# Gate weights carried with the slot rows, and gathers that add into the tokens by DMA, in a graph and mixture-of-experts kernel

## The reference, cut to what matters

```
r      = layernorm(x)
shared = gelu(r @ W1s + b1s) @ W2s + b2s
rw     = softmax(r @ Wr)                        # 8 experts
topw, topi = top_k(rw, 2);  topw /= sum(topw)   # two gate weights per token
routed = sum over the two experts e of topw[e] * (gelu(r @ W1p[e] + b1p[e]) @ W2p[e] + b2p[e])
x      = x + shared + routed
# then: layer norm, two graph attentions of layer 1, last feed-forward stage
```

## Time and profile before

| | |
|---|---|
| median of 3 runs | 1152.54 us (1150.32 to 1153.1) |
| the profiled execution | 1151.04 us |
| its span, first to last instruction | 1149.3 us |
| PE, DVE, ACT, POOL busy | 85%, 66%, 59%, 41% of the span |
| mean granted TensorE clock | 0.948 of full speed |
| POOL's 128 gathers | 1.00 us each on POOL |
| DVE's 71 bias additions | 0.424 us each |

### The profile page before, as it was taken

The page is one execution under the profiler, slowest core; times in us unless marked ns, Lnnn a source line. Parts: engine busy times, 40 slices in busy tenths (PEclk is TensorE's granted clock), DMA queues, the critical chain, the costliest instruction groups (busy, mean ns, idle before and its releaser), DMA issues. The chain is left out here.

```text
span 1149.3 us, 25194 instructions
## 1 busy us (share of the span) xinstructions
PE 982.7 (85%) x7932; PEld 817.2 (71%) x7980; DVE 758.6 (66%) x2314; ACT 678.8 (59%) x1670; POOL 476.0 (41%) x474
## 2 busy tenths in 40 slices
PE   1788888888899999999999925888898998559998
PEld 1577777777677799999999913565665665349997
DVE  4689999987551144455455422687887886559998
ACT  5455656654333446666666612786877888457774
POOL 2555555552064564444300056665676632111111
PEclk9889999998899999999999966998999999769999
DMA  7901100001624136766656411110110100001111
GB/s 203 360 2 39 38 37 37 36 30 60 168 71 127 51 109 189 206 197 192 196 173 176 119 46 44 30 33 23 34 32 25 33 10 1 1 0 29 37 37 46
DMA packets 91706, 94.15 MB, mean 82 GB/s; under 512 B 16336, under 2 KB 69712, under 8 KB 90448
## 3 DMA queue, kind: packets, MB, share of 16 engines
q1 hardware_dynamic: 71936, 50.40, 14.0%
q10 hardware_dynamic: 11472, 25.63, 8.0%
q0 software_dynamic: 8192, 16.79, 4.7%
HBM read 52.54 MB, written 33.96 MB: 75 GB/s over the span
## 5 line engine op out<-in xcount | busy, mean ns | idle before, releaser
L1552 POOL DMA_INDIRECT g_y<-slot_rows_out,slots x128 | 128.3, 1002 | 149.3 <-SPq L1981 99.0
L1287 POOL DMA_INDIRECT slot_rows_in<-xn_all,slots x128 | 126.4, 988 | 133.1 <-DMA slot_rows_in<-xn_all,slots 83.9
L1174 ACT ACTIVATE s_hT<-s_hp,expert 128x256 f32<-128x256 f32 x284 | 113.1, 476 | 70.4 <-PE s_hp L1165 61.3
L1187 PE MATMUL s_yp<-w_experts,s_hT 128*128 x1136 | 138.4, 275 | 0.3 <-issue 0.3
L1187 PEld LDWEIGHTS s_yp<-w_experts,s_hT 128*128 128x128 f32 x1136 | 132.9, 192 | 0.7 <-issue 0.6
L1195 DVE TENSOR_TENSOR xnT_all<-s_yp,expert 128x256 f32<-128x256 f32 x71 | 30.1, 424 | 116.2 <-PE s_yp L1187 85.1
L491 DVE SCALAR_TENSOR_TENSOR l_mi<-l_sbc,mT 128x512 bf16<-128x512 f32 x128 | 86.2, 684 | 11.9 <-PE l_sbc L482 9.6
L1163 PE MATMUL s_hp<-e_xh,e_wh 128*128 128x256 f32 x284 | 85.9, 302 | 0.0
L1086 ACT ACTIVATE s_hT<-s_hp,b_shared 128x512 f32<-128x512 f32 x64 | 44.0, 687 | 65.1 <-PE s_hp L1069 54.8
L1165 PE MATMUL s_hp<-e_xh,e_wl 128*128 128x256 f32 x284 | 80.1, 282 | 0.0
L1164 PE MATMUL s_hp<-e_xl,e_wh 128*128 128x256 f32 x284 | 80.1, 282 | 0.0
(11 more groups left out here) (324 smaller groups left out, 2660.2 us busy)
## 6 DMA issues: line engine op xcount, KB each, us to landing
expert<-expert_rows ACTq DMA_DIRECT2D x65, 322.0 KB
slot_rows_in<-zeros SPq DMA_DIRECT2D x9, 1024.0 KB, 12.4
xnT_all<-slot_rows_in SPq DMA_DIRECT2D x71, 128.0 KB
slot_rows_out<-xnT_all SPq DMA_DIRECT2D x71, 128.0 KB
xn_all<-l_xr SPq DMA_DIRECT2D x16, 256.0 KB, 2.3
xnT_all<-l_rT SPq DMA_DIRECT2D x16, 256.0 KB
out_dram<-f_ot SPq DMA_DIRECT2D x16, 256.0 KB, 2.3
w_experts<-in_L_ffn_W2p_dram SPq DMA_DIRECT2D x8, 256.0 KB, 3.8
```

The lines of the kernel that those rows point to most:

```text
L1174: nc.scalar.activation(hT[q % 2][:, c, :], hp[:, c, 0:TILE], ACT.Gelu, bias=wt[q][:, F + c:F + c + 1]).then_inc(s["h_ok"], 1)
L1187: ins = pe.matmul(yp[q % 2][:, h * D:(h + 1) * D], hT[q % 2][:, c, h * P:(h + 1) * P], w2, start=(c == 0 and h == 0), stop=(c == FC - 1), ...
L1287: pool.indirect_dma_start(k.rows_in, bass.IndirectOffsetOnAxis(ap=k.slots[:, c, b:b + 1], axis=0), k.xn[:, b, :], None).then_inc(scattered ...
L1552: pool.indirect_dma_start(y_slot[c][:, b, :], None, k.rows_out, bass.IndirectOffsetOnAxis(ap=k.slots[:, c, b:b + 1], axis=0))\
```

## The change

- **Rows.** A row of `k.xn` and of `slot_rows_in` grows from 128 to 132 elements (`ROW`), 528 bytes. Elements 128 to 130 of a token's row hold its first expert, the difference of its two gate weights, and the second gate weight. The last is memset to 0 on POOL.
- **Weights.** ACT takes the exponential after its first two groups of the shared expert, and DVE computes the weights there, between the prefix product's input and its result.
- **Expert rows.** The fetched expert row gets one more element, the expert's number.
- **Tile loop.** DVE gets two small instructions for each tile (`dve_weights`), which pick for each slot the first or the second weight, and the bias addition becomes two instructions: add into `e_y_sum`, then multiply by the weight into the tile. `sp_load` waits for `y_ok` of the tile that had the buffer before, instead of its transposes.
- **Graph stage.** The gathers add into `k.x` in the DMA. The order is all four first rows of a group, then all four second rows, still with two in flight. `dve_n_combine` and the two row buffers go, and `dve_n_stats` waits for the gathers.

```diff
+ROW = D + 4
-            sp.dma_start(k.xn[:, bass.ds(g * GB, GB), :], xr[:]).then_inc(s["xr_kept"], 16)
+            sp.dma_start(k.xn[:, bass.ds(g * GB, GB), 0:D], xr[:]).then_inc(s["xr_kept"], 16)
-    k.zero_dmas = 9
+    k.zero_dmas = -(-72 * 2 * ROW // 2048)
-FETCHED = F + FC + D
+FETCHED = F + FC + D + 1
...
-            wait(sp, s["tp_ps"], t - U + 1)
+            wait(sp, s["y_ok"], t - U + 1)
...
+        def dve_weights(dve, i, q):
+            t = i * U + q
+            wait(dve, x_in[q], i * 16 + 16)
+            wait(dve, w_in[q], i * 16 + 16)
+            wait(dve, s["y_ok"], t)
+            dve.scalar_tensor_tensor(of_first[:], xt[q][:, :, D], wt[q][:, FETCHED - 1:FETCHED], xt[q][:, :, D + 1],
+                                     ALU.is_equal, ALU.mult).then_inc(s["weigh"], 1)
+            wait(dve, s["weigh"], 2 * t + 1)
+            dve.tensor_tensor(w_slot[:], of_first[:], xt[q][:, :, D + 2], ALU.add).then_inc(s["weigh"], 1)
+
         def dve_bias(dve, i, q):
             t = i * U + q
             wait(dve, s["y_ps"], t + 1)
+            dve.tensor_tensor(y_sum[:], yp[q % 2][:, 0:H * D].rearrange("p (h d) -> p h d", h=H),
+                              wt[q][:, F + FC:F + FC + D].unsqueeze(1).to_broadcast([P, H, D]), ALU.add)\
+                .then_inc(s["y_sum"], 1)
             wait(dve, out[q], i * 16)
-            dve.tensor_tensor(yt[q], yp[q % 2][:, 0:H * D].rearrange("p (h d) -> p h d", h=H),
-                              wt[q][:, F + FC:FETCHED].unsqueeze(1).to_broadcast([P, H, D]), ALU.add)\
+            wait(dve, s["weigh"], 2 * t + 2)
+            wait(dve, s["y_sum"], t + 1)
+            dve.tensor_tensor(yt[q], y_sum[:], w_slot[:].unsqueeze(2).to_broadcast([P, H, D]), ALU.mult)\
                 .then_inc(s["y_ok"], 1)
...
+            dve_weights(dve, i, q)
             dve_bias(dve, i, q)
...
+                pool.memset(k.xn[:, :, D + 3:ROW], 0.0)
...
+                act.wait_ge(s["lead"], 1)
+                nc.scalar.activation(lead[:], lead[:], ACT.Exp).then_inc(s["lead_exp"], 1)
...
+                dve.tensor_copy(k.xn[:, :, D], which[:, 0])
+                dve.wait_ge(s["lead_exp"], 1)
+                fold(dve.tensor_scalar(share[:], lead[:], 1.0, None, ALU.add))
+                fold(dve.reciprocal(share[:], share[:]))
+                fold(dve.tensor_tensor(k.xn[:, :, D + 2], lead[:], share[:], ALU.mult))
+                dve.tensor_tensor(k.xn[:, :, D + 1], share[:], k.xn[:, :, D + 2], ALU.subtract)
...
+                dve.tensor_copy(k.b_experts[:, :, FC + D], em8[:])
...
-        y_slot = [sb(f"y{c}", [P, BATCHES, D]) for c in range(TOPK)]
...
-                pool.indirect_dma_start(y_slot[c][:, b, :], None, k.rows_out,
-                                        bass.IndirectOffsetOnAxis(ap=k.slots[:, c, b:b + 1], axis=0))\
-                    .then_inc(gathered[g % 2][c], 16)
+                pool.indirect_dma_start(k.x[:, b, :], None, k.rows_out,
+                                        bass.IndirectOffsetOnAxis(ap=k.slots[:, c, b:b + 1], axis=0),
+                                        compute_op=ALU.add).then_inc(gathered[g % 2][lane], 16)
...
-            if on["n"]:
-                dve_n_combine(dve, g + 4, half + 2, p, 0)
             if on["b"]:
                 dve_b_rden(dve, g + 2)
-            if on["n"]:
-                dve_n_combine(dve, g + 4, half + 2, p, 1)
```

More of the change, by code:

```diff
@@ L814, in _ @@
                 for c in range(k.zero_dmas):
-                    sp.dma_start(rows[:, 2048 * c:2048 * c + 2048], k.zeros[:]).then_inc(k.slots_zeroed, 16)
+                    at = slice(2048 * c, min(2048 * c + 2048, 72 * 2 * ROW))
+                    sp.dma_start(rows[:, at], k.zeros[:, 0:at.stop - at.start]).then_inc(k.slots_zeroed, 16)
                 sp.wait_ge(k.slots_zeroed, 16 * k.zero_dmas)
@@ L917, in add_expert_buffers @@
     k.expert_rows = nc.dram_tensor("expert_rows", [EXPERTS, P, FETCHED], F32, kind="Internal").ap()
-    k.b_experts = buffer(nc, ctx, "b_experts", [P, EXPERTS, 4 + 128])
-    k.expert = [buffer(nc, ctx, f"expert{q}", [P, 512 + 4 + 128]) for q in range(6)]
+    k.b_experts = buffer(nc, ctx, "b_experts", [P, EXPERTS, FETCHED - F])
+    k.expert = [buffer(nc, ctx, f"expert{q}", [P, FETCHED]) for q in range(6)]
     k.expert_in = [ctx.enter_context(nc.semaphore(f"expert_in{q}")) for q in range(6)]
@@ L973, in experts_phase @@
         top = sb("r_top", [P, 2, BATCHES])
+        lead, share = sb("r_lead", [P, BATCHES]), sb("r_share", [P, BATCHES])
         which = sb("r_which", [P, 2, BATCHES])
@@ L1006, in experts_phase @@
         wt, w_in = k.expert, k.expert_in
-        xt = [k.xnT[:, H * q:H * q + H, :] for q in range(U)]
-        yt = [k.xnT[:, H * (U + q):H * (U + q) + H, :] for q in range(U)]
+        slot_rows = k.xnT[:].rearrange("p b t -> p (b t)")
+        XT, YT = H * ROW, H * D
+        xt = [slot_rows[:, q * XT:q * XT + XT].rearrange("p (h d) -> p h d", h=H) for q in range(U)]
+        yt = [slot_rows[:, U * XT + q * YT:U * XT + q * YT + YT].rearrange("p (h d) -> p h d", h=H) for q in range(U)]
+        y_sum, of_first, w_slot = sb("e_y_sum", [P, H, D]), sb("e_of_first", [P, H]), sb("e_w_slot", [P, H])
         xh, xl = [[sb(f"e_x{c}{p}", [P, TILE], F32R) for p in range(2)] for c in "hl"]
@@ L1021, in experts_phase @@
             "sh_ps", "sh_ok", "sy_ps", "sy_read", "fold",
-            "tp_ps", "xh_ok", "xT_ok", "wh_ok", "wl_ok", "h_ps", "h_ok", "y_ps", "y_ok")}
+            "lead", "lead_exp", "weigh", "y_sum", "tp_ps", "xh_ok", "xT_ok", "wh_ok", "wl_ok", "h_ps", "h_ok", "y_ps", "y_ok")}
         rows_kept = sem("m_rows_kept")
@@ L1368, in _ @@
                 chain(dve.tensor_reduce(top[:, 1], left, AX.X, ALU.max))
-                dve.tensor_tensor(k.weights[:, 1], top[:, 1], top[:, 0], ALU.subtract)
+                dve.tensor_tensor(lead[:], top[:, 1], top[:, 0], ALU.subtract).then_inc(s["lead"], 1)
                 fold(dve.tensor_tensor(cand, left, over_experts(top[:, 1]), ALU.is_equal))
@@ L1531, in combine_graph_phase @@
             "r2T_ps", "av2_ps", "q2_ok", "v2_ok", "v2_cut", "w2_ok", "t2_ok", "s2_ok", "x_ok", "stats4", "var4", "kept4")}
-        gathered = [[sem(f"gathered{p}{c}") for c in range(TOPK)] for p in range(2)]
-        w_exp, w_share = sem("w_exp"), sem("w_share")
-        share = sb("share", [P, BATCHES])
+        gathered = [[sem(f"gathered{p}{lane}") for lane in range(2)] for p in range(2)]
         def full(count, g, ahead):
@@ L1546, in pool_gather, with dve_n_stats @@
             for n in which:
[L1547 to L1568 removed]
+                c, b, lane = n // GB, g * GB + n % GB, n % 2
+                if n < 2:
+                    wait(pool, gathered[1 - g % 2][lane], 16 * GB * ((g + 1) // 2))
+                else:
+                    wait(pool, gathered[g % 2][lane], 16 * (GB * (g // 2) + n // 2))
+                pool.indirect_dma_start(k.x[:, b, :], None, k.rows_out,
+                                        bass.IndirectOffsetOnAxis(ap=k.slots[:, c, b:b + 1], axis=0),
+                                        compute_op=ALU.add).then_inc(gathered[g % 2][lane], 16)
+        def dve_n_stats(dve, g, half, p):
+            for lane in range(2):
+                wait(dve, gathered[p][lane], (half + 1) * 16 * GB)
             dve.memset(fence[:], 0.0)
@@ L1960, in dve_slot @@
             if on["n"]:
-                dve_n_stats(dve, g + 4, p)
+                dve_n_stats(dve, g + 4, half + 2, p)
             if on["e"]:
@@ L1983, in _ @@
             def _(dve):
-                dve.wait_ge(w_exp, 1)
-                dve.tensor_scalar(share[:], k.weights[:, 1], 1.0, None, ALU.add).then_inc(w_share, 1)
-                dve.wait_ge(w_share, 1)
-                dve.reciprocal(k.weights[:, 0], share[:]).then_inc(w_share, 1)
-                dve.wait_ge(w_share, 2)
-                dve.tensor_tensor(k.weights[:, 1], k.weights[:, 1], k.weights[:, 0], ALU.mult).then_inc(w_share, 1)
-                dve.wait_ge(w_share, 3)
                 slots(dve_slot, dve)
@@ L1995, in _ @@
                 exp_ln_tables(nc, act)
-                nc.scalar.activation(k.weights[:, 1], k.weights[:, 1], ACT.Exp).then_inc(w_exp, 1)
                 slots(act_slot, act)
```

28 lines of the change are left out of this document (6 added, 22 removed).

## The result

The changed kernel takes 1181.94 us (median of 4 runs, 1180.76 to 1186.93), the kernel before 1152.82 in the same comparison: ratio 1.0269, 95% interval 1.0237 to 1.0302, +29 us. The stated range held it; the time named was 13 us too low, and the narrower band of its leading case, 1158 to 1178 us, missed it. Measured again for experiment 5, the same pair stands at 1188.95 to 1131.98, ratio 1.0506 (1.0465 to 1.0547), +57 us: the changed kernel takes much the same (+7 us), the kernel before is 21 us faster. What differs is told with the experiments.

A forecast was written before the change was run, and what follows sets the result against it. PE was taken to bound the tile loop, POOL's 32 gathers the ramp, a loop through POOL the slots. 0 + 3.7 + 0.5 + 11.2 - 1 + 3 = +17.4 on 1151.0, taken as 1169 us; range 1144 to 1192.

The forecast's parts named there:

- leading case: Likeliest case, chance 0.46: each pair of gathers takes 0.35 to 0.9 us more, giving 1158 to 1178 us.
- step 4: Ramp of the graph stage: accumulating gathers take longer, 0.7 us more a pair, 16 pairs, +11.2 us.
- Rival B: Gathers get no longer because the DMA pipelines the addition; 1151 to 1157 us, chance 0.20.
- step 5: Steady slots of the graph stage: DVE relief -1 us, POOL's 2.6 us a slot exceeding slack in narrow slots +3 us.
- rival C: Heavy gathers, a pair +1.0 us or more: ramp +16, slots +10, tile loop +4, 1181 us; chance 0.17.
- DVE's relief: Steady slots: DVE loses about 3.1 us of work a slot, but only 0.1 us of it shortens the slot, -1 us.
- Rival D: Faster: DVE's 3.1 us a slot are on the path after all, 1142 us; chance 0.17.
- step 3: Tile loop: DVE's spare time holds the new work; 8 pauses grow, +3.7 us, last tile +0.5, later loads 0.
- step 2: Scatters of 528-byte rows: at most about 4 us more over all, hidden by 11 us before the loads are needed, 0.
- The case that I left to the tail: Scatters: longer rows cost 10% instead of three per cent, 26 us, so the loads come 15 us late.
- Routing chain: Weights computed before the graph stage: DVE's 1.3 to 1.8 us and ACT's exponential hidden in idle time, 0.
- A: The forecast case, chance 0.46, likeliest time 1169 us; mean slot 18.2 to 18.5 us, ramp about 55 us.

The follow-up runs named there:

- experiment 5: The kernel before and the changed kernel run again without edit, beside each other on one chip: 1131.98 and 1188.95 us, ratio 1.0506.

## Why the forecast was right in its sign and 13 us too low

*Ramp (step 4): right place, mis-sized, other mechanism.* I wrote that "a pair takes 0.7 us more", from a longer transfer. It takes 0.9 more, 3.70 us for 2.77 on the ramp's average (the 2.69 that I read was one short pair), and it is POOL's work: 1.54 + 0.30 a gather. The time from issue to landing rose from 2.5 to 3.3 us in the two kernels on one chip, and 0.59 of this 0.8 is POOL's longer instruction, so the data path itself accounts for about 0.2. Two gathers in flight would now allow 3.3 us a pair; POOL needs 3.70. In my sum the 0.35 "for more work in POOL's descriptors" was a side term, halved because the other gather would hide it; it was the whole and hides nothing once POOL is the bound. Rival B's reason held and its time did not: the Trainium skill's rule ("DMA: Bandwidth & Descriptors", anatomy of one DMA), that most of the fixed time is the write's receipt, fits the small 0.2 us of the data path. The same section calls the generation of descriptors small. POOL's instruction, which holds it if the packets above are its work, went from 0.95 to 1.54 us here and decided.

*Slots (step 5): the term that failed most.* The "2.6 us a slot" of slack was misread: the lines of the earlier trace rows hold for 820 to 900 us, some 4.5 slots, and the whole window from 800 on has 10.0 us in 5 and 9.2 in 6 waits, 3.5 us a slot. It was also partly made of the pauses of that profile; in experiment 5 the two waits come to 1.9 us a slot (13.4 us from 760 to 880 us). And the extra work is 8 x 0.59 = 4.7 us of POOL's time, all of it, not 2.6. POOL's sum 18.6 against a loop of 16.7 makes +1.9 a slot where there are no pauses (+26 in 15 slots), and +0.6 where there are (266.6 / 15 = 17.8 against 18.4: +9 measured, +2 forecast). This was rival C's mechanism, which I gave 0.17: POOL's loop becomes the bound. Its ramp of +16 and its slots of +10 stand near the measured 14.4 and 9.0. That its time of 1181 met the first measurement is in part luck, since it had 4 us for the tile loop where the profile has 11.3.

*DVE's relief: right.* The last two slots of the kernel before have neither gathers nor combinations and still take 16.54 to 16.68 us in both of its profiles, where most undisturbed full slots take 16.7 to 16.8; so DVE's 3.1 us less work could give some 0.1 to 0.2 us a slot. Rival D falls with this. Removing DVE's additions couldn't pay.

*Tile loop (step 3): a wrong path, and too little.* "Each of 8 pauses grows" by 0.46 us: where there are no pauses, the same work costs +7.6 us, and in the profile PE loses its time at the last fence. The later release of the loads, "0", costs some 4 us more. Of +11.3 us to the first gather in the first profile I had 4.2.

*Scatters (step 2): wrong.* "0" rested on 11 us of lead; it is 3 to 7. The case that I left to the tail, rows that cost more than their bytes, is the real one at a smaller size: +10 us by the medians.

*Routing chain, end of kernel: right*, nothing to be seen there beyond 1 us.

*The signs.* A mean slot of 18.4 us and PE's 22.26 us in the window from 495 us came as named for A. Missed were POOL's time for a gather (1.61 us, not 1.00), PE's window from 570 us (20.29, not 25.00), the last fence (584 us, not 568) and PE's wait at the ramp (17.86 us, not 23: PE's work ahead of it ended 42.2 us after the first gather, where it had been 32.7). The mean slot was met because the 18.16 us of the kernel before already held pauses. So the sign was right, and the time was near only where they were there: in experiment 5 +17 us would stand against +57.

## What to carry to other kernels

Cost a DMA on the engine that issues it as well as on its way: an option such as accumulation can cost more on GpSimd's program than it saves on VectorE, and where gathers stand ahead of arithmetic in GpSimd's order, each 0.6 us counts. Before calling a later transfer free, measure the one fence that everything behind it waits for, by its distance to the next stage in several runs. A slack read from one profile may be the shadow of that execution's pauses: take it from the tightest slots. And before a late fence in one profile is put down to an edit, see how late it comes in a kernel without the edit.

## What the runs showed of the hardware

- An accumulating gather of 128 rows of 512 bytes makes 144 packets instead of 32, keeps GpSimd 1.54 us instead of 0.95, and lands 3.3 us instead of 2.5 after its start.
- VectorE takes longer while GpSimd computes beside it. The leaky step (L1669) takes 2.66 us on average in the changed kernel's slots, where it begins 1.1 us after GpSimd's residual of 2.9 us, and 0.73 in the first profile of the kernel before, where it begins 2.4 us after it (923.78 and 921.38 in the earlier trace rows). In one slot of the kernel before in experiment 5 four combinations take 1.11 us (from 784.89), and the four behind them 2.00 us (from 786.15), with GpSimd's scaling of 1.04 us from 786.38. The first four ran beside a gather (784.69 to 785.70) and weren't slowed by it. What the two engines share no run isolates. The rows are those of the grouped view, of the changed kernel in experiment 5 and of the kernel before:

```profile
L1669 DVE SCALAR_TENSOR_TENSOR g_e<-g_sum 128x512 f32<-128x512 f32 x10 | 26.6, 2658 | 12.9 <-ACT g_sum L1662 12.9
```
```profile
L1652 DVE SCALAR_TENSOR_TENSOR g_e<-g_sum 128x512 f32<-128x512 f32 x12 | 8.8, 731 | 23.7 <-ACT g_sum L1645 23.7
```

- The kernel before differs by 21 us between the first measurement and the later ones on two chips, and its two profiles differ by pauses that no record explains, while the changed kernel takes 7 us more when measured again. Whether the chip or the hour makes it is open.
- Slot rows of 528 bytes in place of 512 cost this kernel 10.0 us, and VectorE work that stays within its spare time in the tile loop cost 7.6 us. In both profiles TensorE loses its time once, at the last fence of the scatters. A scatter of 128 rows makes 32 packets at 512 and 528 bytes and 48 at 768.
